# Convolution rows loaded by transfers that lead with 32 partitions, and layer normalisation of images 2 to 8 moved beside the scan

## What is computed

```python
# stage 1: depthwise 17x17 convolution, pointwise mix, gate per channel and image
h = bn1(x); h = depthwise_conv17(h); h = gelu(bn2(einsum('bchw,dc->bdhw', h, pw)))
a = sigmoid(relu(h.mean((2, 3)) @ w1.T + b1) @ w2.T + b2)
x1 = x + gamma * h * a[:, :, None, None]
# stage 2: layer norm over the 96 channels of each of 4096 tokens, then a Mamba block
xn = (x1 - mean) * rsqrt(var + 1e-5) * ln_g + ln_b          # (8, 4096, 96)
u, z = split(xn @ W_in); u = silu(causal_conv4(u)); dt, B, C = project(u)
h_t = exp(dt_t * A) * h_{t-1} + dt_t * B_t * u_t;  y_t = h_t . C_t + u_t * D
out = (y * silu(z)) @ W_out                 # scanned forwards and backwards, y summed
```

## Time and profile before

| | us |
|---|---|
| median of 3 runs | 5559.85 (5557.4 to 5569.05) |
| the profiled execution | 5567.16, span of its trace 5565.3 |
| busy: DVE / POOL / PE / ACT | 5198.8 / 4820.8 / 4537.5 / 3300.4 |
| convolution: first matmul to last DVE instruction | 40.85 to 354.14 |
| normalise: first DVE add to its last instruction | 467.50 to 612.83 |
| scan: first load of a pass to the last DVE instruction | 616.79 to about 5518 |

### The profile page before, as it was taken

One profiled execution on the slowest core, in us unless ns is written; L12 is line 12 of the kernel. 1 busy time (PEld: TensorE's weight loads), 2 busy tenths in 40 slices (PEclk: granted clock), 3 DMA queues, 4 the chain that ended last, 5 costly groups with the idle time before them and its releaser, 6 DMA issues. The chain is left out here.

```text
span 5565.3 us, 77050 instructions
## 1 busy us (share of the span) xinstructions
PE 4537.5 (82%) x18064; PEld 1235.1 (22%) x18064; DVE 5198.8 (93%) x3757; ACT 3300.4 (59%) x5416; POOL 4820.8 (87%) x2295
## 2 busy tenths in 40 slices
PE   5878578878888888888888888888888888888887
PEld 4553111111222112122111212211122211112222
DVE  5556489999999999999999999999999999999998
ACT  1237556656666666666666666666666666666665
POOL 0020189999999999999999999999999999999998
PEclk9999777777888888888888888888888888888887
DMA  2237555565666666666666666666666666666666
GB/s 75 75 94 235 171 168 183 186 199 191 210 195 195 200 208 208 200 206 198 195 201 209 204 202 203 198 196 201 213 198 208 197 200 198 202 214 195 211 196 203
DMA packets 365956, 1062.76 MB, mean 191 GB/s; under 512 B 71396, under 2 KB 119926, under 8 KB 315340
## 3 DMA queue, kind: packets, MB, share of 16 engines
q1 hardware_dynamic: 355724, 1045.89, 58.2%
q10 hardware_dynamic: 8064, 14.16, 0.8%
q0 software_dynamic: 1984, 1.06, 0.1%
HBM read 849.20 MB, written 211.63 MB: 191 GB/s over the span
## 5 line engine op out<-in xcount | busy, mean ns | idle before, releaser
L1476 POOL TENSOR_TENSOR hc<-hring,c_rep 128x1024 f32<-128x1024 f32 x1541 | 3604.2, 2364 | 82.0 <-DVE hring L1431 78.8
L1431 DVE TENSOR_TENSOR_SCAN hring<-decay,carry,u_ps 128x1024 f32<-128x1024 f32 x1157 | 2670.3, 2331 | 0.0
L1413 DVE TENSOR_TENSOR u_ps<-u_ps,u_rep 128x1024 f32<-128x1024 f32 x1157 | 1396.4, 1207 | 86.0 <-DMA u_rep<-u_scr 65.0
L1171 PE MATMUL u_ps<-stack_b,w_spread 48*128 48x512 bf16 x2314 | 856.0, 455 | 717.6 <-DVE hring L1431 713.2
L1303 ACT ACTIVATE decay<-dt_rep,w_a 128x1024 f32<-128x1024 f32 x1158 | 1325.5, 1145 | 122.4 <-DVE hring L1431 108.9
L1189 PE MATMUL y_ps<-hc,w_gather 128*32 128x512 f32 x6144 | 1036.9, 754 | 0.0
L1303 ACT ACTIVATE u_ps<-dt_rep,w_a 128x1024 f32<-128x1024 f32 x386 | 430.6, 1116 | 1008.4 <-DVE hring L1431 1004.4
L1463 POOL TENSOR_TENSOR drive_p<-u_rep,b_rep 128x1024 f32<-128x1024 f32 x386 | 912.3, 2364 | 12.1 <-DMA u_rep<-u_scr 12.1
L1431 DVE TENSOR_TENSOR_SCAN hring<-u_ps,carry,drive_p 128x1024 f32<-128x1024 f32 x385 | 900.5, 2339 | 0.0
L1171 PEld LDWEIGHTS u_ps<-stack_b,w_spread 48*128 48x128 bf16 x2314 | 134.2, 98 | 1915.2 <-DVE hring L1431 1601.8
L1212 PE MATMUL prep_ps<-xn,w_conv 128*128 128x512 f32 x792 | 459.5, 694 | 121.9 <-ACT xc L1326 95.9
(11 more groups left out here) (152 smaller groups left out, 4398.6 us busy)
## 6 DMA issues: line engine op xcount, KB each, us to landing
dt_rep<-dt_scr SPq DMA_DIRECT2D x194, 1024.0 KB, 5.9
u_rep<-u_scr SPq DMA_DIRECT2D x194, 1024.0 KB, 6.3
c_rep<-bc_scr SPq DMA_DIRECT2D x260, 512.0 KB, 4.7
b_rep<-bc_scr SPq DMA_DIRECT2D x130, 512.0 KB, 5.8
xn<-xn_scr SPq DMA_DIRECT2D x132, 384.0 KB, 5.3
y_scr<-y_sb SPq DMA_DIRECT2D x768, 64.0 KB, 1.9
xn<-xn_scr SPq DMA_DIRECT2D x132, 256.0 KB, 4.7
dt_scr<-dt_sb SPq DMA_DIRECT2D x260, 128.0 KB, 2.1
```

What stands on the lines that cost most here:

```text
L1171: mm = nc.tensor.matmul(u_ps[nv % NSLOT][:, sl], w["spread"][:, q, :], upper(stack_b[drv][:, sl]), start=True, stop=True)
L1413: nc.vector.tensor_tensor(slot[:, :], slot[:, :], u_rep[r][:, b, :], ALU.mult).then_inc(drive_ready, 1)
L1431: nc.vector.tensor_tensor_scan(hring[nv % NHR][:, ::step], factor[:, ::step], term[:, ::step], carry[:, drv, nv:nv + 1], ALU.mult, ALU.add ...
L1476: nc.gpsimd.tensor_tensor(hc[nv % NHC][:, :], hring[nv % NHR][:, :], c_rep[q][:, :], ALU.mult).then_inc(c_applied, 1)
```

## The change

1. `load` in the convolution: six transfers instead of eight. Each has the rows of one parity as its first dimension (32 rows, or 24 at the image's edge); the two cells whose rows adjoin go in one transfer, whose second dimension is the cell. Margins outside the image now hold rows of the other parity, and are multiplied by zero as before.
2. `normalise` does the 8 slices of image 1 only.
3. A new task `norm` in `scan` normalises one slice of 512 tokens in each of the 56 passes of images 1 to 7, for the image after: SP loads at step 5, ACT scales `centrer` by the gate at 10, PE multiplies 4 blocks of 128 tokens (tokens now on partitions) at 11 and 12, ACT copies out at 13, squares at 14 and scales at 15, PE turns the blocks back at 20, ACT applies gain and bias at 21, SP stores at 22. It also uses `prep_ps`.
4. The order of the users of `prep_ps` changes: the second y sum goes from step 10 to 2, projection, copy out and store from 12, 13, 14 to 10, 11, 12, the first z from 20 to 21. Waits follow: the first dt matmul waits for DVE's second product.

```diff
-                rows = d["x_cols"].rearrange("(a y) c b x -> a y (c b x)", a=2)
+                rows = d["x_cols"].rearrange("r c b x -> r (c b x)")
-                    def put(p, q, a, lo, n):
-                        sp.dma_start(xraw[buf][p:p + n, q, :], rows[a, lo:lo + n, cols]).then_inc(x_in[buf], 16)
-                    put(PAD, 0, 0, 0, ROWS)
...
-                    for q in range(1, NCY - 1):
-                        lo = q * CY - PAD
-                        sp.dma_start(xraw[buf][:, q, :], rows[:, lo:lo + ROWS, cols]).then_inc(x_in[buf], 16)
...
+                    n = ROWS - PAD
+                    for a in range(2):
+                        to = xraw[buf][ROWS * a:ROWS * (a + 1), :, :]
+                        q0, q1 = 1 - a, 2 - a
+                        first = H * a + q0 * CY - PAD
+                        sp.dma_start(to[:, q0:NCY:2, :], rows[first:first + 2 * ROWS, cols].rearrange("(q y) n -> y q n", q=2)).then_inc(x_in[buf], 16)
+                        first = H * a + q1 * CY - PAD
+                        sp.dma_start(to[:, q1, :], rows[first:first + ROWS, cols]).then_inc(x_in[buf], 16)
+                    sp.dma_start(xraw[buf][PAD:ROWS, 0, :], rows[0:n, cols]).then_inc(x_in[buf], 16)
+                    sp.dma_start(xraw[buf][ROWS:ROWS + n, NCY - 1, :], rows[2 * H - n:2 * H, cols]).then_inc(x_in[buf], 16)
...
-                over_slices(dve, (5, add), (1, scale), (0, shift))
+                over_first(dve, (5, add), (1, scale), (0, shift))      # 8 slices; so on each engine
...
-        SLICE_AT, Z_AT = 15, (20, 22)
-        SUM_Y_AT, PROJECT_AT, RES_AT, OUT_STORE_AT = (0, 10), 12, 13, 14
+        SLICE_AT, Z_AT = 15, (21, 22)
+        SUM_Y_AT, PROJECT_AT, RES_AT, OUT_STORE_AT = (0, 2), 10, 11, 12
+        NORM_IN_AT, NORM_GATE_AT, CENTRE_AT, TOKENS_AT, SQUARE_AT, SCALE_AT = 5, 10, (11, 12), 13, 14, 15
+        TURN_AT, NORM_OUT_AT, NORM_STORE_AT = 20, 21, 22
...
# SP, norm: wait centred; dma gate_now (96 x 1), nh <- act_scr, nx <- x_tok (96 x 512 each);
#           step 22: wait norm_out; dma xn_scr <- nout (96 x 512). SP, conv step 0: wait norm_stored
# PE
+                            if g == 0 and beside[1]:
+                                pe.wait_ge(tokens_out, pn - 1)                        # first conv matmul
...
+                        if g == 0 and beside[0]:
+                            pe.wait_ge(gated, 2 * (pn - 1 - OUT_LAG) + 2)             # first dt matmul
...
+                        if norming:
+                            pe.wait_ge(norm_out, k + OUT_LAG)                         # first z
...
+                        pe.wait_ge(prep_out, NPREP * (k + OUT_LAG + 2))               # projection
...
+                def norm(m, p, it, dr, slicing):
+                    if m == CENTRE_AT[0]:
+                        pe.wait_ge(norm_in, 48 * (p + 1)); pe.wait_ge(centrer_gated, p + 1)
+                        pe.wait_ge(res_ready, p - OUT_LAG + 1)                        # if slicing
+                    for j in range(NBLK):
+                        if m == CENTRE_AT[j // 2]:
+                            to, tok = prep_ps[:, j * C:(j + 1) * C], slice(j * P, (j + 1) * P)
+                            nc.tensor.matmul(to, nh[:, tok], gated_centrer[:, :], start=True, stop=False)
+                            mm = nc.tensor.matmul(to, nx[:, tok], w["centrer"][:, :], start=False, stop=True)
...
+                    if m == TURN_AT:
+                        pe.wait_ge(tokens_scaled, p + 1); pe.wait_ge(prep_out, NPREP * (p + 2) + 3)
+                        for j in range(NBLK):
+                            mm = nc.tensor.matmul(prep_ps[0:C, j * P:(j + 1) * P], ntok[:, j, :], w["ident"][:, :], start=True, stop=True)
...
# ACT, norm (between slice and conv in a step's order)
+                        nc.scalar.activation(gated_centrer[:, :], w["centrer"][:, :], ACT.Copy, scale=gate_now[:, 0:1])
+                        nc.scalar.copy(ntok[:, :, :], prep_ps[:, 0:NBLK * C]...)          # 128 x 384
+                        for j in range(NBLK):                                             # step 14
+                            mm = nc.scalar.activation(squares[:, j, :], ntok[:, j, :], ACT.Square, accum_out=nstat[:, 0, j:j + 1])
+                        # step 15: Ln and Exp of 128 x 4, each waiting for the one before, then
+                        for j in range(NBLK):
+                            mm = nc.scalar.activation(ntok[:, j, :], ntok[:, j, :], ACT.Copy, scale=nstat[:, 2, j:j + 1])
+                        nc.scalar.activation(nout[:, :], prep_ps[0:C, :], ACT.Identity, bias=w["lng"][:, 1:2], scale=w["lng"][:, 0:1])
```

More of the change, by code:

```diff
@@ L100, in over_slices, with over_first @@
     image(B - 1, last=True)
+def over_first(eng, *stages):
+    most = max(lead for lead, _ in stages)
+    for s in range(-most, NS):
+        for lead, what in stages:
+            if 0 <= s + lead < NS:
+                what(0, s + lead)
 def over_last(eng, *stages):
@@ L799, in scan @@
         res = sb("res", [C, SL])
+        nh = sb("nh", [C, SL])
+        nx = sb("nx", [C, SL])
+        gated_centrer = sb("gated_centrer", [C, C])
+        gate_now = sb("gate_now", [C, 1])
+        nstat = sb("nstat", [P, 3, NBLK])
+        neps = sb("neps", [P, 1])
+        ntok = sb("ntok", [P, NBLK, C])
+        squares = sb("squares", [P, NBLK, C])
+        nout = sb("nout", [C, SL])
         u_ps = [ctx.enter_context(nc.psum_tensor(f"u_ps{i}", [P, 2 * SL], F32)) for i in range(NSLOT)]
@@ L1022, in front, with conv @@
                         load_u(*later(3, u, n, it, dr))
-                def conv(m, pn, it, dr, slicing):
+                def conv(m, pn, it, dr, beside):
                     if m == XN_AT:
+                        counts = (16 * (pn - 1) if beside[1] else 16 * (NORM_PASSES + 1), NPREP * (pn - 1) + 3)
+                        stored, done = ready(*counts)
                         it = it if isinstance(it, int) else it % ITERS
-                        wait(sp, prep_done, NPREP * (pn - 1) + 3, not isinstance(pn, int) or pn > 0)
+                        wait(sp, prep_done, done, not isinstance(pn, int) or pn > 0)
+                        wait(sp, norm_stored, stored, not isinstance(pn, int) or pn > 1)
                         for tap, lo, hi, j, at in TAP_ROWS:
@@ L1030, in conv, with prep @@
                             sp.dma_start(xn[at:at + hi - lo, j, :], d["xn_scr"][it // CHUNKS, lo:hi, bass.ds(first, T)]).then_inc(xn_in, 16)
-                def prep(m, pn, it, dr, slicing):
+                def prep(m, pn, it, dr, beside):
                     first = isinstance(pn, int) and pn == 0
@@ L1391, in _ @@
                 act.wait_ge(zeroed, 1)
                 load_exp_ln(nc)
-                run(act, ("back", back), ("prep", prep), ("slice", slice_out), ("conv", conv), ("gate", gate), ("front", front))
+                run(act, ("back", back), ("prep", prep), ("slice", slice_out), ("norm", norm), ("conv", conv), ("gate", gate), ("front", front))
             @block.vector
@@ L1635, in vision_mixer_kernel @@
                 pointwise(nc, d, hs, gate, w)
-            normalise(nc, d, gate)
-        scan(nc, d, w)
+            normalise(nc, d, gate, w)
+            scan(nc, d, w, gate)
     output(nc, d)
```

144 lines of the change are left out of this document (104 added, 40 removed).

## The result

| | median us | ratio to before (95% interval) |
|---|---|---|
| before | 5563.49 (5557.4 to 5569.05) | |
| changed kernel | 5527.99 (5527.71 to 5530.65) | 0.9938 (0.992 to 0.9955) |

What follows compares the result with a forecast made beforehand. It took the convolution as bound by its transfers' shape, normalise by ACT and DVE nearly full, the scan by DVE. -76 - 4 - 121 + 20 = -181 us from 5567.2 gave 5386, or 5379 against the median; range 5342 to 5445.

Steps and rivals of the forecast that it cites:

- Loads, -76 - 4: Convolution: faster loads bring a batch to 9.8 us, saving 76 us, and an earlier start saves 4 us.
- Rival C: Convolution: loads do not speed up because two-cell transfers stay narrow; 5459 us, chance 0.07.
- Normalise, -121: Normalise: 56 of 64 slices leave the block, saving 121 us.
- Part 3: Scan: one slice per pass in 56 of 64 passes, its throughput hidden in idle time of ACT and PE.
- The scan, +20: Scan: late spreads from the new `prep_ps` order cost 0.35 us in each of 56 passes, 20 us; bounds 0 and 84.
- steps 2 to 4: Scan pass: the spread of step 4 has 0.3 us of room, no stall; 1 us late at the half clock.
- 10 to 12: Scan pass, these steps: 2 to 3 us more on PE at the full clock, with room of about 0.5 to 2 us.
- Steps 5 to 8: Scan pass: a 2.2 us delay runs down the dt chain, ACT makes up some; 0 to 1.1 us of stall.
- rival B: Scan loses 1 to 1.5 us a pass at steps 4 to 8, waiting for the second product; 5415 to 5443 us, chance 0.15.
- Steps 15 to 17: Scan pass: convolution and spreads come 1.2 us later; room at the full clock, up to 2 us late at the half clock.
- A: Rival for the scan: the same savings with nothing lost there, -201 us, 5359 us, chance 0.25.
- D: Rival for the scan: the `prep_ps` chain becomes longer than a pass, slower than before; 5639 us at 80 us a pass, chance 0.05.

Runs made afterwards that it cites:

- the loads alone: The kernel before with only the convolution's new six-transfer load: 5475.61 us, ratio 0.9841.
- both moves: The changed kernel with ACT copying the convolution's first third at step 14 and DVE's second product between step 2's drive and scan: 5368.23 us, ratio 0.9648.
- the second product's move: The changed kernel with DVE's second product of the gate between the drive and scan of step 2 instead of behind both: 5437.42 us, ratio 0.977.
- the fillers: The changed kernel with two zero-weight matmuls added into `y_ps` on PE at step 15 of every pass: 5464.35 us, ratio 0.9828.
- the scalings at step 18: The changed kernel with the slice's Ln, Exp and four scalings on ACT at step 18 instead of 15: 5441.74 us, ratio 0.9782.
- the early copy: The changed kernel with ACT copying out the convolution's first third at step 14, ahead of that step's decay, instead of step 15: 5442.49 us, ratio 0.978.

## Why the prediction was wrong

- **Loads, -76 - 4.** Right, and a little low: -89 for the loads alone. The rows of the last batch gave 9.8 us with the handing over to ACT in it; a batch took 9.47, PE with no gap, a little under the lower bound of 9.6. DVE, with 7.46 us of work a batch, waits 48 us for PE in all and nothing for `xraw`.
- **Transfers.** From 100 to 110 us of the changed kernel each slice with traffic moves 82 to 475 GB/s, and the stretch of 50 GB/s is gone. The Trainium skill's rule (DMA: Bandwidth & Descriptors, why a DMA increments its semaphore by 16) agrees with that. Rival C falls.
- **Normalise, -121.** Right: -123.
- **Part 3, throughput of the added work hidden.** Right: DVE waits for no `dt_rep`, `u_rep` or decay. One of the prediction's signs of being wrong did come: POOL's idle time grew with DVE's (busy 4060.26 of 4280 us, 4176.80 of 4240 before). It does not show that POOL holds DVE back: POOL's waits for DVE's scans grew from 58.7 to 184.0 us, and no wait of DVE in the scan is for POOL. Only "hidden" was taken to mean "free where it stands".
- **The scan, +20: the step that failed.** Its size was 173 us; the bound of 84 was too low as well. Of the four spots, steps 2 to 4 (no stall) and 10 to 12 (room) came out as said. *Steps 5 to 8* were put at 0 to 1.1 us and then taken near nothing, because "ACT, with 37% idle, makes up some of the delay". It does not, since from the second dt matmul on the chain is PE's own row of work at the half clock. With no slice beside it the order costs 81 us, 1.4 in each of the 56 passes with a slice of output. That is rival B's mechanism, at its place and price. *Steps 15 to 17* were said to have room "at full clock", with the clock of the kernel before, where the half level was there in 23 of 100 passes. The same sentence had the 1.2 us by which the copy comes later (1.6 by the rows) and the 2 us that it would cost at the half clock. What it lacked was that the one brings on the other: PE idles 3.3 in place of 1.7 us, and the clock falls in nearly every pass. That costs 85.5 us when taken away and 95 when put in by itself.
- **"Three of four places have room by the rows"** took a mean over places for a size. The two that had none cost 1.4 to 1.8 us each in each pass. Mending them gave 85.5 and 90.6 us by itself and 160 together, of the 175 lost, so one stall hardly makes room for the other, as the prediction had assumed.
- **Rivals.** With both moves the kernel comes within 9 us of A (5359, nothing lost in the scan). B held for one of two places. D did not happen: the pass is longer by the waits at two places, and taking these away gives 75.0 to 75.7 us, so the chain on `prep_ps` is not closed.

What is left open: what makes the half clock come in one pass and not in another when the gap is shorter than 2.66 us; why the second product's move also shrinks the waits of steps 16 and 17; what the fillers' new waits at step 0 come from; and where the 15 us lie by which both moves stay above 5353. None of these was followed.

## What to carry to other kernels

An engine's idle share says what added work costs in throughput, and nothing of what it costs where it stands: ask of each added instruction which instruction behind it on its engine has someone waiting, and how long that one then idles. When the one that idles is TensorE, price the work behind the gap at the half clock, and not at the clock that the kernel before had there; it costs only where someone waits for that work. A delay at the head of a stretch in which the next engine has no gap arrives whole at its end; here a 0.4 us instruction put before a scan and not behind it was worth 90 us.

## What was not expected of the hardware

- With a gap of 1.68 us of TensorE (the loads alone) the clock stayed at 1.00 in about three of four passes; with a gap of 2.66 to 3.41 us it fell to 0.50 in all or nearly all, and two matmuls of work without use (1.88 us) that cut the gap to 1.60 us kept it at 1.00 in 92 of 100 and made the kernel 64 us faster. They are worth having only where the gap itself can't be removed: removing it gave 85 us.
- The length of that gap does not decide alone. With 1.68 us again (the scalings at step 18) the half level came in 54 of 100 passes, and with 2.15 us a little elsewhere (the early copy) in 62; neither made VectorE wait.
- A batch of the convolution ran 9.47 us, with TensorE busy in all of it for over 200 us at clock 1.00.
